# Flamingo-style gated block on one core: one Sinkhorn run for two batches, close output tiles in the tail, the next scores in mid unit

## The reference

```python
# attention: windows of 128 columns, 8 heads of 32, D = 512, DK = 256
q = Wq @ layernorm(x) + bq;  k = Wk @ layernorm(x) + bk;  v = Wv @ ctx + bv
o = gelu(softmax(q.k / sqrt(32)) v)               # per window and head
x = x + tanh(g_xattn) * (Wo @ o + bo) * mask
# ffn: each of the 512 rows of a batch has 2048 columns = 4 streams of 512
y = layernorm(x);  y_norm = y * rsqrt(mean(y*y) + eps)
H_res  = sinkhorn((y_norm @ W_res.T) + base, 50 iterations, tau = 0.1)   # 4 x 4 a row
H_pre, H_post = softmax(y_norm @ W_pre.T + ..), softmax(y_norm @ W_post.T + ..)
H_res = (1 - g) * I + g * H_res
out = H_res @ streams(y) + H_post * ((H_pre . streams(y)) @ W_branch)
x = x + tanh(g_ffn) * out
```

## Time and profile before

| | us |
|---|---|
| median of 3 runs | 1916.64 (1911.25 to 1918.87) |
| the profiled execution | 1918.8 |
| its span, first to last instruction | 1917.0 |
| PE busy | 1458.7 (76%) |
| DVE busy | 1346.0 (70%) |
| POOL busy | 995.8 (52%) |
| ACT busy | 943.2 (49%) |
| mean granted TensorE clock | 0.915 |

### The profile page before, as it was taken

The page is one execution under the profiler, slowest core; times in us unless marked ns, Lnnn a source line. Parts: engine busy times, 40 slices in busy tenths (PEclk is TensorE's granted clock), DMA queues, the critical chain, the costliest instruction groups (busy, mean ns, idle before and its releaser), DMA issues. The chain is left out here.

```text
span 1917.0 us, 35771 instructions
## 1 busy us (share of the span) xinstructions
PE 1458.7 (76%) x12548; PEld 880.6 (46%) x12704; DVE 1346.0 (70%) x3486; ACT 943.2 (49%) x1889; POOL 995.8 (52%) x1653
## 2 busy tenths in 40 slices
PE   2777989988988888888888888889888965424244
PEld 0544556555555555555554555555455542211011
DVE  3443445777788878887888788877777777676654
ACT  2355666655655555654656465556555543211011
POOL 4433445556566656665566656666666343433311
PEclk9888999999999999998999999999999977656676
DMA  7455776657666566665666566665555433321122
GB/s 246 138 158 162 202 197 172 174 152 205 181 187 191 160 190 193 182 184 152 178 188 184 162 177 188 190 180 166 158 160 162 122 89 88 88 71 61 44 99 77
DMA packets 173922, 299.89 MB, mean 156 GB/s; under 512 B 23568, under 2 KB 74640, under 8 KB 169648
## 3 DMA queue, kind: packets, MB, share of 16 engines
q1 hardware_dynamic: 147120, 230.48, 39.8%
q0 software_dynamic: 26624, 67.12, 15.1%
HBM read 179.81 MB, written 67.11 MB: 129 GB/s over the span
## 5 line engine op out<-in xcount | busy, mean ns | idle before, releaser
L1173 DVE TENSOR_REDUCE ssum<-kp 128x16 f32<-128x64 f32 x768 | 182.8, 238 | 209.6 <-POOL kp L543 206.9
L842 ACT ACTIVATE probs<-st_ps,key_bias 128x512 f32<-128x512 f32 x256 | 174.2, 681 | 226.6 <-PE st_ps L737 224.1
L543 POOL TENSOR_TENSOR kp<-ke,sv 128x64 f32<-128x64 f32 x376 | 166.7, 443 | 222.9 <-DVE sv L1174 219.5
L543 POOL TENSOR_TENSOR kp<-ke,sa 128x64 f32<-128x64 f32 x392 | 116.3, 297 | 298.0 <-DVE sa L1174 298.0
L1047 DVE TENSOR_REDUCE negm<-s_ps 128x4 bf16<-128x512 f32 x256 | 168.5, 658 | 141.3 <-PE s_ps L723 140.4
L630 PE MATMUL pr<-x_hl,wq 128*128 128x512 bf16 x707 | 175.3, 392 | 44.8 <-POOL x_hl L459 37.7
L644 PE MATMUL pr<-wv,ctx_hl 128*128 128x256 bf16 x1536 | 176.4, 273 | 33.6 <-DVE k_hl L1032 20.2
L657 PE MATMUL pr<-o_sb,wo 128*128 128x512 bf16 x705 | 175.0, 386 | 29.9 <-DVE x1c L1064 26.2
L464 POOL TENSOR_TENSOR ctx_hl<-ctx_raw,ctx_hl 128x512 bf16<-128x512 f32 x128 | 165.4, 1296 | 59.3 <-ACT ctx_hl L804 59.3
L459 POOL TENSOR_TENSOR x_hl<-xc,x_hl 128x512 bf16<-128x512 f32 x128 | 148.0, 1168 | 57.0 <-ACT x_hl L810 56.8
L630 PE MATMUL pr<-x_hl,wk 128*128 128x512 bf16 x736 | 173.7, 386 | 2.1 <-issue 0.5
(11 more groups left out here) (146 smaller groups left out, 3307.1 us busy)
## 6 DMA issues: line engine op xcount, KB each, us to landing
xs<-in_dram SPq DMA_DIRECT2D x128, 256.0 KB, 6.0
xc<-in_dram SPq DMA_DIRECT2D x32, 1024.0 KB, 6.9
ctx_raw<-in_dram SPq DMA_DIRECT2D x32, 1024.0 KB, 5.5
x1c<-in_dram POOLq DMA_DIRECT2D x64, 512.0 KB, 6.2
x_dram<-x1c SPq DMA_DIRECT2D x32, 1024.0 KB, 5.1
out_dram<-otile POOLq DMA_DIRECT2D x64, 512.0 KB, 3.9
q_st<-q_hl SPq DMA_DIRECT2D x384, 64.0 KB
k_st<-k_hl SPq DMA_DIRECT2D x384, 64.0 KB
```

The costliest lines, as they stand in the source:

```text
L543: nc.gpsimd.tensor_tensor(kp[:], ke[:], v, ALU.mult).then_inc(kp_made, 1)
L842: nc.scalar.activation(probs[:, k % 2, :], st_ps[:], ACT.Exp, bias=key_bias[:, b, w:w + 1], scale=SCALE).then_inc(exp_done, 1)
L1173: cf.link(nc.vector.tensor_reduce(s_t, k, AX.X, ALU.add))
```

## The change

1. `ke`, `kp`, `sa`, `sv` and `ssum` get room for two batches. There are nine runs: run r does the first 50 halves (iterations 1 to 25) of batch r and at the same time the last 48 (26 to 49) of batch r-1, in one instruction for both where both take part (`in_run`, `of_run`). A run starts at step 32(r+1)+22 and takes 12.5 steps; the last, for batch 7 alone, starts at step 293. `coefficients(r-1)` comes behind half 47 of run r. `rb`, `pre` and `post` get three buffers, `pre` an own semaphore.
2. Tiles of batches 0 to 4 keep their parts and start 16 steps later (32(f+1)+70+8t). Those of batches 5, 6 and 7 start at steps 262, 291 and 315, six steps apart, with other offsets (`BEHIND`). They have no diagonal matrices and no `mix`: ACT starts row 3 too and DVE adds its streams, 3 + 12 + 4 operations of DVE.
3. The stores are issued by SP and not by POOL.
4. PE makes the scores of unit g+1 in step g, behind the first of the step's banks (or at the end where there is none), and not those of g at its start.
5. DVE does its second half and all tile work ahead of `divide`; POOL does its second scaling ahead of the splits and its third behind them; the diagonals are made three steps earlier.

```diff
+EARLY, LATE = 2 * RETURN, 2 * (ITERS - 1 - RETURN)
+RUNS = B + 1
+RUN_AT = [UNITS * (r + 1) + SINK_AT for r in range(B)]
+RETURN_AT = SINK_AT + EARLY // 4
+RUN_AT.append(RUN_AT[-1] + EARLY // 4 + 3)
+BESIDE = dict(load=-7, first=-5, xpre=-2, pre=-1, branch=0, diag=-4, mix=1, out_0=0, out_1=1,
+              stream_1=1, y=2, stream_2=3, stream_3=4, pair_1=5, store_0=5, store_1=6)
+BEHIND = dict(load=-7, first=-5, xpre=-4, pre=-3, branch=-2, out_0=-1, out_1=1,
+              stream_1=0, stream_2=1, y=2, stream_3=3, pair_1=4, store_0=4, store_1=5)
+MIXED = B - 3
+TILE_AT = {(f, t): UNITS * (f + 1) + 70 + UPC * t for f in range(MIXED) for t in range(DT)}
+for _f, _first in zip(range(MIXED, B), (NU + 6, NU + 35, NU + 59)):
+    TILE_AT.update({(_f, t): _first + 6 * t for t in range(DT)})
...
+def halves(r):
+    return EARLY if r < B else LATE
+def run_at(g, part):
+    for r in range(RUNS):
+        n = 4 * (g - RUN_AT[r]) + part
+        if g >= RUN_AT[r] and n < halves(r):
+            return r, n
+    return None
+def in_run(r, n):
+    return [f for f, last in ((r - 1, LATE), (r, EARLY)) if 0 <= f < B and n < last]
...
-        ke = sb("ke", [P, DT, N, N])
-        kp = sb("kp", [P, DT, N, N])
+        ke = sb("ke", [P, 2, DT, N, N])
+        kp = sb("kp", [P, 2, DT, N, N])
...
         # SP, at the end of a step
+                for done, t in tiles_at(g, "store_0"):
+                    store(done, t, 0)
+                for done, t in tiles_at(g, "store_1"):
+                    store(done, t, 1)
         # POOL
-                nc.gpsimd.tensor_tensor(kp[:], ke[:], v, ALU.mult).then_inc(kp_made, 1)
+            def scale(r, n):
+                pool.wait_ge(scale_made, halves_before(r) + n)
+                v = bcast(of_run(sa, r, n), 3, N) if n % 2 else bcast(of_run(sv, r, n), 2, N)
+                nc.gpsimd.tensor_tensor(of_run(kp, r, n), of_run(ke, r, n), v, ALU.mult).then_inc(kp_made, 1)
+                scale_at(g, 1)
                 if 0 <= G - 1 < NG and r == 4:
                     for et in range(ET):
                         low_gelu(G - 1, et)
                 for H, t in at_step(g, -2, LOW_X_AT):
                     split_x(H, t)
-                scale_at(f, its, 1)
                 for H, t in at_step(g, -2, NORM_AT):
                     norm_x(H, t)
-                scale_at(f, its, 2)
                 for H, t in at_step(g, -1, LOW_CTX_AT):
                     split_ctx(H, t)
+                scale_at(g, 2)
-                for done, t in tiles_at(g, 5):
-                    store(done, t, 0)
-                for done, t in tiles_at(g, 6):
-                    store(done, t, 1)
         # PE
-                if 0 <= g < NU:
-                    scores(g)
                 if 0 <= g - 1 < NU:
                     scores_t(g - 1)
                 if 0 <= g - 2 < NU:
                     values(g - 2)
-                for what in banked_at(g):
+                made = banked_at(g)
+                for n, what in enumerate(made):
...
+                    if n == 0 and 0 <= g + 1 < NU:
+                        scores(g + 1)
+                if not made and 0 <= g + 1 < NU:
+                    scores(g + 1)
         # ACT
-                for done, t in tiles_at(g, 1):
-                    first_out(done, t, 2)
+                for done, t in tiles_at(g, "out_1"):
+                    for i in range(2, N - 1 if done < MIXED else N):
+                        first_out(done, t, i)
         # DVE
+            def half_iteration(r, n):
+                if n:
+                    dve.wait_ge(kp_made, halves_before(r) - r + n)
+                else:
+                    answered()
+                k = of_run(kp if n else ke, r, n)
...
+                cf.link(nc.vector.tensor_reduce(total, k, AX.X, ALU.add))
+                nc.vector.reciprocal(of_run(sv if n % 2 else sa, r, n), total).then_inc(scale_made, 1)
+                if n == LATE - 1 and r:
+                    dve.wait_ge(scale_made, halves_before(r) + LATE)
+                    coefficients(r - 1)
...
-                if 0 <= g - 2 < NU:
-                    divide(g - 2)
-                half_at(f, its, 1)
-                for k, j in ((1, 1), (3, 2), (4, 3)):
-                    for done, t in tiles_at(g, k):
-                        add_stream(done, t, j, (0, 1))
-                for done, t in tiles_at(g, 2):
-                    add_y(done, t)
-                for done, t in tiles_at(g, 5):
-                    for j in range(1, N):
-                        add_stream(done, t, j, (2,))
-                for done, t in tiles_at(g, -2):
-                    make_xpre(done, t)
-                half_at(f, its, 2)
+                half_at(g, 1)
+                for j in range(1, N):
+                    for done, t in tiles_at(g, f"stream_{j}"):
+                        add_stream(done, t, j, (0, 1))
+                for done, t in tiles_at(g, "y"):
+                    add_y(done, t)
+                for done, t in tiles_at(g, "pair_1"):
+                    for j in range(1, N):
+                        add_stream(done, t, j, (2,) if done < MIXED else (2, 3))
+                for done, t in tiles_at(g, "xpre"):
+                    make_xpre(done, t)
+                if 0 <= g - 2 < NU:
+                    divide(g - 2)
+                half_at(g, 2)
```

More of the change, by code:

```diff
@@ L89, in ffn_at, with tiles_at, halves_before @@
     return [f] if (g - e) % UNITS == 0 and 0 <= f < B else []
[L92 to L103, removed]
+def tiles_at(g, part):
+    return [(f, t) for (f, t), at in TILE_AT.items()
+            if part in (BESIDE if f < MIXED else BEHIND) and g == at + (BESIDE if f < MIXED else BEHIND)[part]]
+def halves(r):
+    return EARLY if r < B else LATE
+def halves_before(r):
+    return sum(halves(i) for i in range(r))
+def run_at(g, part):
[6 more added lines that the diff above has]
+    return [f for f, last in ((r - 1, LATE), (r, EARLY)) if 0 <= f < B and n < last]
 def stat_steps(b):
@@ L124, in banked_at @@
     made += [("sel", f, 0) for f in ffn_at(g, UPC + SELECT_AT)]
-    made += [("pre", f, t) for f, t in tiles_at(g, -1)]
-    made += [("mix", f, t) for f, t in tiles_at(g, 1)]
+    made += [("pre", f, t) for f, t in tiles_at(g, "pre")]
+    made += [("mix", f, t) for f, t in tiles_at(g, "mix")]
     if 0 <= G + 1 < NG:
@@ L326, in program @@
         y_read = sem("y_read")
+        pre_ready = sem("pre_ready")
         coef_ready = sem("coef_ready")
@@ L386, in load_x1t, with store @@
                 sp.dma_start(x1t[n % 2][:], x1dr[f, :, t, :]).then_inc(x1t_loaded[n % 2], 16)
+            def store(f, t, pair):
+                sp.wait_ge(out_ready, f * (2 * DT) + 2 * t + pair + 1)
+                half = slice(2 * pair * C, 2 * (pair + 1) * C)
+                sp.dma_start(outr[f, t, :, half], otile[:, 2 * pair:2 * pair + 2, :].rearrange("p n c -> p (n c)")
+                               ).then_inc(out_stored[pair], 16)
             def stack(G, dst, blocks):
@@ L426, in _ @@
                     load_xs(*later)
-                for f, t in tiles_at(g, -7):
+                for f, t in tiles_at(g, "load"):
                     load_x1t(f, t)
@@ L445, in _ @@
                     load_mask(G + 3)
+                for done, t in tiles_at(g, "store_0"):
+                    store(done, t, 0)
+                for done, t in tiles_at(g, "store_1"):
+                    store(done, t, 1)
+            for pair in range(2):
+                sp.wait_ge(out_stored[pair], 16 * DT * B)
         @block.gpsimd
@@ L492, in add_x @@
                                accum_op=ALU.add).then_inc(x1_added[h], 16)
-            def store(f, t, pair):
-                pool.wait_ge(out_ready, f * (2 * DT) + 2 * t + pair + 1)
-                half = slice(2 * pair * C, 2 * (pair + 1) * C)
-                pool.dma_start(outr[f, t, :, half], otile[:, 2 * pair:2 * pair + 2, :].rearrange("p n c -> p (n c)")
-                               ).then_inc(out_stored[pair], 16)
             cp = Chain(pool, pool_chain)
@@ L519, in stat_b @@
             def stat_b(f, part):
[L520 removed]
+                r = rb[:, f % 3]
                 if part == 0:
@@ L1182, in half_at @@
-            def half_at(f, its, part):
-                it, half = its[part // 2], part % 2
-                if it is not None:
-                    half_iteration(f, it, half)
+                fs = in_run(r, n)
+                total = ssum[:] if len(fs) == 2 else ssum[:, fs[0] % 2:fs[0] % 2 + 1]
+                total = total.rearrange("p s (t i) -> p (s t) i", t=DT)
+                cf.link(nc.vector.tensor_reduce(total, k, AX.X, ALU.add))
+                nc.vector.reciprocal(of_run(sv if n % 2 else sa, r, n), total).then_inc(scale_made, 1)
```

140 lines of the change are left out of this document (63 added, 77 removed).

## The result

The changed kernel takes 1919.4 us in the median (1914.2 to 1933.5, 20 runs), the kernel before 1914.1 us (1907.8 to 1918.9, 20 runs); the ratio is 1.0041, 95% interval 1.0025 to 1.0057. The two medians are 5.3 us apart; the ratio, which goes over all the runs, makes it some 8 us slower, where 15 us less were forecast. The two profiled executions hide this: their spans are 1916.1 and 1917.0 us, that of before being above its median.

What follows compares the result with a forecast made beforehand. A DVE and POOL chain that PE waits for, PE close behind, was taken to bound the steady part; in the tail engines take turns. Terms -1 - 7 - 15 + 8 = -15 us gave 1904 profiled, 1902 median; range 1845 to 1942.

Steps and rivals of the forecast that it cites:

- The +2 us on the products: Units 22 to 34 of a steady batch: some twenty products that DVE waits for cost 2 us more.
- Batches 0 to 2: First three batches: about -7 us in batch 2, whose tiles start later, and -1 for batches 0 and 1.
- A: Units 3 to 16 of a middle batch: Sinkhorn leaves, PE's own pace stays; -5 us (ends 0 and 11.7).
- the tail: From the end of attention: three stretches at -20, +29 and -1 us, together +8 us.
- the last stretch: Third stretch of the tail, the last tiles at 17.6 us each: 98 us, a change of -1.
- B: Units 22 to 34 of a middle batch: wide halves, partly absorbed by DVE's 6.3 us score waits; +3 us (ends 0, +10.5).
- The five steady batches: Batches 3 to 7: -3 us a batch, -15 us in all.
- +8.5: Units 22 to 34 of a steady batch: 50 halves, now wide, add 8.5 us of DVE work.
- Late quotient: Steady batches: `divide` moved behind the tile work, taken at nothing and kept as a rival.
- scores -1 a batch: Steady batches: next scores in mid unit take DVE's few score waits; -1 us a batch (ends -6 and +3).
- Late divide: Rival, chance 0.18, slower: `divide` behind tile work delays PE in units with tile work; 1930 to 1957 us.
- The stores: Units 22 to 34 of a steady batch: POOL no longer issues stores, -1 us a batch.

Runs made afterwards that it cites:

- e13: Kernel before with its output stores issued by SP instead of POOL, nothing else: 1908.5 us, ratio 0.9964.
- e10: Changed kernel with both edits of order undone (quotient early, scores at the start of the step): 1938.2 us, ratio 1.0134.
- e6_narrow: Changed kernel with the late half iterations left out, so each Sinkhorn run works on one batch, 64 elements wide: 1861.4 us, ratio 0.9737.
- e11: Changed kernel with four x1t buffers in the tail, two halves a step in the steady batches and later output tiles: 1836.1 us, ratio 0.9600.
- e9_before_both: Kernel before with only the two edits of order, late quotient and scores in mid unit: 1907.2 us, ratio 0.9968.

## Why the prediction was wrong

**The sizes were nearly right.** Reciprocals 353 ns (forecast 0.35 us), products 413 ns (0.42), reductions 331 ns in the mean (0.31): in the median 286 for the plain one (0.30) and 376 for the strided one (0.31), which I had too short. The +2 us on the products that DVE waits for did not come: 12.4 us after, 12.3 before. A slowed product grew from 794 to 859 ns at the longest, that is by 0.07 us, not to 1.1 us in proportion. This agrees with what the Trainium skill gives, "SBUF — State Buffer", section "SBUF: two separate sides": a port held for one whole instruction adds its wait once.

**Batches 0 to 2 and A were right, the tail nearly.** Measured alone, in the table of `e13` and `e10`, they are -8.5, -5.0 and +6.2 us, forecast -8, -5 and +8. The last tiles take 18.0 us (17.6) and the last stretch 97.6 us (98). Against the kernel before the whole tail came out at +1.5 only: the moved stores gave it 4.6, which I had put at nothing.

**The step that failed is B's sum in "The five steady batches"**: "the 6.3 us in which DVE waited for PE absorb as much", which made +3 of +8.5, +2 and -1. Next to nothing was absorbed. `e10_sink_tail`, the new Sinkhorn in the old order of work, shows it: DVE still waits 5.8 us for scores in B, where it waited 6.3, and B is longer by 14.8 us with 14.5 us more of DVE's work. (In the changed kernel these waits are down to 0.9 us, but there the edits of order took them, and PE's waits for DVE grew by more: `o_sb` from 3.2 to 12.1 us, `negm` from 2.4 to 7.2.) `e6_narrow` takes the width away and B falls by 8.5 us, all of the +8.5 that I had.

The lengths of the units bear out the reason: the idle time stood in few places, the halves are in every unit. DVE's longest score wait, 3.3 us, falls into unit 22. That unit takes 8.3 us in `e13` and in `e10`, and its wait is 1.9 us in the latter: there the slack did cover the work. The twelve other units of B are each longer, by 0.2 to 3.0 us, and together make up the whole difference; PE, two units deep at most, did not win it back in the one with slack. Three things that I had left out of B add to it: tile work slower by 3.2 us; the coefficients, 2.0 us, which I had charged to the tail and to nothing else; and the clock. In the Bs read here the granted clock is 1.00 where PE idles 3.1 us (`e11`), 0.98 at 10.0 (before), 0.96 at 13.6 (`e6`), 0.93 at 19.4 (after) and 0.89 at 17.0 (`e10`): mostly lower where PE pauses more. That the pauses cause it is argued and not isolated. Together the five batches came out 36 us longer where 5 less were forecast.

**The trade was misjudged as a whole.** What A lost in DVE work was worth only 5 us, as forecast, since PE is at its pace there; what B gained cost 15. How many halves stand in one step mattered more than the number of instructions saved: with the same wide halves in all, two a step instead of four, batch 6 takes 190.5 us instead of 206.8. That lever, which the kernel had in its tables, I never priced.

**The edits of order.** Late quotient 0 and scores -1 a batch, -5 together. On the kernel before they give 6 us together, but that this meets my sum is luck: the late quotient alone loses 5 and the scores alone 31. In the changed kernel the pair gives 18 (1.0134 to 1.0041). The rival "Late divide" was wrong in sign for the pair: the quotient is late for PE (its `o_sb` waits rose from 42.9 to 99.5 us in all), but its early place costs far more once scores come in mid unit. I priced the two edits apart, and they cannot be.

**The stores.** -1 a batch, -5: measured 7 us on the kernel before, and 20 in the changed one. The sum was near and the places were not: on the kernel before, 1 us of it is in the five steady batches and 4.6 in the tail.

**The sum by parts**, in points of the time of before: stores -0.36, Sinkhorn and tail +1.70, orders -0.93, together +0.41, that is -7, +33, -18 and +8 us; forecast -5, -5, -5 and -15.

## What to carry to other kernels

Two engines that wait for each other in turns have no common store of slack: price added work unit by unit, and count idle time as cover only in the very units where the work is put. When work is made fewer but wider, its placing has to be thinned at the same time: here the same instructions were worth +8 us at four a step and, with the tail's buffers, -83 us at two or three. Edits of order that meet at one wait are to be tried together and apart, since either alone can lose what both gain.

## What was not expected of the hardware

- In the last tiles of the changed kernel a load of 1 MB and a store of 0.5 MB beside each other land after 5.8 and 6.7 us; the median of its twelve stores there is 2.6 us. Two more buffers, which let the loads run ahead, save 3.5 us a tile.
- DVE's three-operand instructions over 512 elements took 767 to 862 ns in B before and 962 to 1204 ns after, with POOL busy 60% of the stretch before and 59% after. The width of the products is not the cause: with narrow ones (`e6_narrow`) they take 962 to 1254 ns. Nor are the two edits of order, since `e10_sink_tail`, without them, has the same slowness and `e9_before_both`, with them alone, has not. What is left is the rest of the change, POOL's new order of work among it, and no run isolates that. With two halves a step (`e11_two_a_step`) the additions to `otile` are back at 827 to 867 ns, those to `xpre` stay at 1172.
- To issue a store of 0.5 MB costs POOL itself 0.62 us of busy time.
